# U of the gated layer made in the layer's row blocks, and two bfloat16 parts made by ScalarE

## What is computed

```
Wh = x @ W_w + W_b
Uh = x @ U_w + U_b
Vh = x @ V_w + V_b
out_src = Wh * attn_l
out_dst = Wh * attn_r
sigma = jax.nn.sigmoid(out_src[src] + out_dst[dst])
sum_sigma_h = jax.ops.segment_sum(Vh[src] * sigma, dst, num_segments=N)
sum_sigma = jax.ops.segment_sum(sigma, dst, num_segments=N)
h = Uh + sum_sigma_h / (sum_sigma + 1e-06)
```

## Time and profile before

| | us |
|---|---|
| median of 3 runs | 3004.75 (3004.15 to 3007.91) |
| the profiled execution | 3003.86, its span 3002.2 |
| input stage, first gather to last subtraction | 1639.3 to 1732.8 |
| gather stage, first gather to last store | 1738.4 to 2817.9 |
| last stage | 2830.0 to 3002.2 |

### The profile page before, as it was taken

One profiled execution on the slowest core, in us unless ns is written; L12 is line 12 of the kernel. 1 busy time (PEld: TensorE's weight loads), 2 busy tenths in 40 slices (PEclk: granted clock), 3 DMA queues, 4 the chain that ended last, 5 costly groups with the idle time before them and its releaser, 6 DMA issues. The chain is left out here.

```text
span 3002.2 us, 50772 instructions
## 1 busy us (share of the span) xinstructions
PE 2495.9 (83%) x17111; PEld 1245.4 (41%) x17164; DVE 2350.3 (78%) x5375; ACT 1158.3 (39%) x2327; POOL 1364.5 (45%) x1627
## 2 busy tenths in 40 slices
PE   5999979999969999966997947677676777767598
PEld 3666655333355333344665512233332333323365
DVE  6888889999959999977444847777777777777477
ACT  5777720000020000012222435666666666566421
POOL 2999920000000000001830867777777777775055
PEclk8999989999989999976998977888888888888799
DMA  4000000000020000031432687888888888888343
GB/s 125 12 11 12 10 36 15 15 15 15 5 82 15 15 15 15 5 100 45 121 96 64 203 249 238 250 259 256 259 255 252 257 257 260 255 252 250 121 150 107
DMA packets 210756, 373.53 MB, mean 124 GB/s; under 512 B 52554, under 2 KB 140559, under 8 KB 208682
## 3 DMA queue, kind: packets, MB, share of 16 engines
q0 software_dynamic: 75536, 238.14, 26.4%
q1 hardware_dynamic: 131737, 128.66, 13.5%
q10 hardware_dynamic: 3200, 3.21, 0.4%
HBM read 324.84 MB, written 50.04 MB: 125 GB/s over the span
## 5 line engine op out<-in xcount | busy, mean ns | idle before, releaser
L1167 PE MATMUL dense_p_o<-dense_W,feat 128*32 128x512 f32 x7200 | 789.8, 595 | 17.5 <-DVE dense_W L1099 17.5
L1099 DVE SCALAR_TENSOR_TENSOR dense_W<-layer_B,steep,cnt 128x512 f32<-128x512 f32 x1200 | 796.7, 750 | 3.3 <-DVE dense_W L1099 2.0
L2466 POOL DMA_INDIRECT Wd<-tab_d,ixq x544 | 519.4, 955 | 171.1 <-issue 166.2
L1167 PEld LDWEIGHTS dense_p_o<-dense_W,feat 128*32 128x32 f32 x7200 | 281.9, 110 | 494.5 <-issue 390.3
L1577 POOL MEMSET edst<- 128x782 int32 x1 | 0.8, 750 | 921.9 <-POOLq L1216 921.9
L2644 PE MATMUL strips_p_sg<-strips_sv,strips_oh 128*32 128x512 f32 x2000 | 313.6, 704 | 101.0 <-DVE strips_sv L2509 101.0
L2632 PE MATMUL strips_p_b<-strips_wrs,strips_ohT 96*128 96x256 bf16 x1000 | 177.8, 308 | 208.8 <-DVE strips_ohT L2480 190.6
L732 POOL TENSOR_SCALAR mix_L<-mix_back,encode_lowT 128x128 bf16<-128x128 f32 x520 | 328.6, 650 | 18.7 <-PE mix_p_c L891 18.6
L2573 ACT ACTIVATE strips_p_s<-strips_tv 128x1024 f32<-128x1024 f32 (+1 forms) x250 | 225.2, 901 | 157.3 <-DVE strips_sv L2509 144.5
L1123 ACT COPY dense_part<-dense_p_o 128x512 f32<-128x512 f32 x36 | 18.8, 596 | 639.7 <-PE dense_p_o L1167 639.7
L2466 POOL DMA_INDIRECT strips_G<-tab_d,ixq x240 | 228.9, 954 | 73.1 <-issue 72.8
(11 more groups left out here) (543 smaller groups left out, 3899.3 us busy)
## 6 DMA issues: line engine op xcount, KB each, us to landing
strips_row<-dlr_d SPq DMA_DIRECT2D x250, 96.0 KB
ew<-in_ew SPq DMA_DIRECT2D x16, 1024.0 KB, 5.4
layer_B<-rise_d SPq DMA_DIRECT2D x12, 1024.0 KB, 4.6
hx_d<-hrow SPq DMA_DIRECT2D x24, 512.0 KB, 2.7
Wd<-tab_d,ixq POOLq DMA_INDIRECT x544
Wd<-in_fWd SPq DMA_DIRECT2D x8, 1024.0 KB, 9.2
tab_d<-feat SPq DMA_DIRECT2D x50, 130.0 KB, 1.9
tab_d<-gated_in_rowg SPq DMA_DIRECT2D x25, 256.0 KB, 2.0
```

Of the source, the lines that this page charges most:

```text
L1099: o = nc.vector.scalar_tensor_tensor(out=out, in0=rise, scalar=C.steep[:, q * H + h:q * H + h + 1], in1=count, op0=ALU.max, op1=ALU.mult)
L1167: m = nc.tensor.matmul(p_o[c % 2][h * MT:(h + 1) * MT, a, 0:n], feat[:, q, h, lo:lo + MT], W[t % 3][:, h, 0:n], start=(q == 0), stop=(q == ...
L2466: gp.indirect_dma_start(out=G[n % RING][:, j, :], out_offset=None, in_=C.tab3[:, :], in_offset=bass.IndirectOffsetOnAxis(ap=index, axis=0) ...
```

## The change

- **Input stage.** `w3` holds only W and V, loaded in two pieces. U's product, its copy `us` and its store are gone; the second product has 256 columns. The transposed rows `xT` get four buffers and SP stores them to `xT_d` (`turned`), ahead of the block's `row`. VectorE no longer multiplies by attn_r twice. ScalarE makes part 0 by a cast of `wf` (`first_part`, two rounds behind) and part 1 by another cast of `wf` after GpSimd's first subtraction (`second_part`, three rounds behind). GpSimd keeps the two subtractions, each waiting for one of the casts.
- **Gather stage.** `wu` holds U's weights. `project(b)` makes U of block b in the last 256 columns of `p_h`: two matmuls from `xTu` and a bias matmul, on TensorE at the end of the block's steps, behind the gate matmuls of block b-2. VectorE adds it from PSUM. SP loads `xTu` (one buffer) when the product of the block before is done. `xn` has one buffer, the zero matmuls read `b3S` in place of `nil`, and waits keep the last part of `p_h` apart from the hidden layer.
- **The branch not taken** gets a loop that makes U for all blocks.

```diff
-        w3 = sb("w3", [P, KC, 3 * D])
+        w3 = sb("w3", [P, KC, 2 * D])
...
+                def turned(b):
+                    sp.wait_ge(s_tc, b + 1)
+                    sp.dma_start(C.xT_d[ds(b * P, P), :], xT[b % 4][:, :]).then_inc(s_xTd[b % 4], 16)
...
                     k = b % 3
-                    gp.wait_ge(s_row, b * 3 + 3)
+                    gp.wait_ge(s_w0, b + 1)
                     nc.gpsimd.tensor_tensor(wf[k][:, :], wf[k][:, :], wp[k][:, 0, :], ALU.subtract).then_inc(s_sp, 1)
-                    gp.wait_ge(s_sp, b * 3 + 1)
-                    nc.gpsimd.tensor_copy(wp[k][:, 1, :], wf[k][:, :]).then_inc(s_sp, 1)
-                    gp.wait_ge(s_sp, b * 3 + 2)
+                    gp.wait_ge(s_w1, b + 1)
                     nc.gpsimd.tensor_tensor(wp[k][:, 2, :], wf[k][:, :], wp[k][:, 1, :], ALU.subtract).then_inc(s_sp, 1)
...
-                    nc.vector.tensor_tensor(wp[m][:, 0, :], p_a[k][:, 0, 0:D], ar[:, :], ALU.mult).then_inc(s_row, 1)
...
-                    nc.scalar.copy(row[k][:, D:2 * D], p_a[k][:, 1, D:2 * D]).then_inc(s_pass, 1)
-                    nc.scalar.copy(us[k][:, :], p_a[k][:, 1, 0:D]).then_inc(s_pass, 1)
+                    nc.scalar.copy(row[k][:, D:2 * D], p_a[k][:, 1, 0:D]).then_inc(s_pass, 1)
+
+                def first_part(b):
+                    act.wait_ge(s_row, b * 2 + 2)
+                    if b >= 3:
+                        act.wait_ge(s_wd[b % 3], 16 * (b // 3))
+                    nc.scalar.copy(wp[b % 3][:, 0, :], wf[b % 3][:, :]).then_inc(s_w0, 1)
+
+                def second_part(b):
+                    act.wait_ge(s_sp, b * 2 + 1)
+                    nc.scalar.copy(wp[b % 3][:, 1, :], wf[b % 3][:, :]).then_inc(s_w1, 1)
...
-                for b in range(NB + 1):
+                for b in range(NB + 3):
...
-                    if b >= 1:
+                    if 1 <= b <= NB:
                         taken(b - 1, (b - 1) % 2)
+                    if 2 <= b <= NB + 1:
+                        first_part(b - 2)
+                    if b >= 3:
+                        second_part(b - 3)
...
-                    for a, lo, w in ((0, 0, D), (1, D, 2 * D)):
+                    for a, bias in ((0, 0), (1, 2 * D)):
...
                     def load_u(b):
-                        sp.dma_start(U[b % 2][:, :], C.u_d[b * P:(b + 1) * P, :]).then_inc(s_u[b % 2], 16)
+                        if b >= 1:
+                            sp.wait_ge(s_up, b)
+                        sp.dma_start(xTu[:, :], C.xT_d[b * P:(b + 1) * P, :]).then_inc(s_u, 16)
...
-                        if i == 0 and b >= 1 and b + 1 < NB:
-                            sp.wait_ge(s_ur, b)
+                        if i == 8 and 0 <= b and b + 1 < NB:
                             load_u(b + 1)
...
-                            v.wait_ge(s_u[b % 2], 16 * (b // 2 + 1))
+                            v.wait_ge(s_up, b + 1)
                             v.wait_ge(s_d, 4 * b + 2)
-                            nc.vector.tensor_tensor(h, h, U[b % 2][:, :], ALU.add).then_inc(s_ur, 1)
+                            nc.vector.tensor_tensor(h, h, p_h[:, F - D:F], ALU.add).then_inc(s_ur, 1)
...
+                    def project(b):
+                        if b == 0:
+                            pe.wait_ge(s_wu, 16)
+                            pe.wait_ge(s_ones, 1)
+                        else:
+                            pe.wait_ge(s_ur, b)
+                        pe.wait_ge(s_u, 16 * (b + 1))
+                        for kc in range(KC):
+                            nc.tensor.matmul(p_h[:, F - D:F], xTu[:, kc * P:kc * P + P], wu[:, kc, :], start=(kc == 0), stop=False)
+                        nc.tensor.matmul(p_h[:, F - D:F], ones[:, :], C.b3S[:, D:2 * D], start=False, stop=True).then_inc(s_up, 1)
...
+                            if i == QC + 7 and b < NB - 1:
+                                pe.wait_ge(s_ur, b + 2)
...
                             t.then_inc(s_l4, 1)
+                            if b + 2 < NB:
+                                project(b + 2)
                         if i == 2 * QC + 2:
                             pe.wait_ge(s_lt, b + 1)
+                            pe.wait_ge(s_ur, min(b + 3, NB))
```

More of the change, by code:

```diff
@@ L2148, in _ @@
                     sp.wait_ge(s_wd[k], 16 * ((NB + 2 - k) // 3))
+                for k in range(4):
+                    sp.wait_ge(s_xTd[k], 16 * ((NB + 3 - k) // 4))
                 sp.wait_ge(s_dw, 32)
-                sp.wait_ge(s_rowd[0], 32 * ((NB + 1) // 2))
-                sp.wait_ge(s_rowd[1], 32 * (NB // 2))
+                sp.wait_ge(s_rowd[0], 16 * ((NB + 1) // 2))
+                sp.wait_ge(s_rowd[1], 16 * (NB // 2))
             @block.gpsimd
@@ L2654, in group @@
                             for n in range(4):
-                                nc.tensor.matmul(p_sg[g // QC % 2][:, :], nil[:, 0:P], nil[:, :], start=False, stop=False)
+                                nc.tensor.matmul(p_sg[g // QC % 2][:, :], nil[:, :], C.b3S[:, 0:2 * D], start=False, stop=False)
                         sums(g)
+                    def project(b):
[8 more added lines that the diff above has]
+                        nc.tensor.matmul(p_h[:, F - D:F], ones[:, :], C.b3S[:, D:2 * D], start=False, stop=True).then_inc(s_up, 1)
                     def tail(b, i):
+                        if i == 0 and b < 2:
+                            project(b)
                         if i == QC + 4:
@@ L2940, in load_u @@
                         sp.dma_start(U[b % 4][:, :], C.u_d[b * P:b * P + P, :]).then_inc(s_u[b % 4], 16)
+                    sp.dma_start(wu[:, :, :], A["w3"][:, D:2 * D].rearrange("(c p) f -> p c f", p=P)).then_inc(s_wu, 16)
+                    for b in range(NB + 1):
+                        if b < NB:
+                            if b >= 2:
+                                sp.wait_ge(s_up, b - 1)
+                            sp.dma_start(U[b % 2][:, :], C.xT_d[b * P:b * P + P, :]).then_inc(s_ux[b % 2], 16)
+                        if b >= 1:
+                            sp.wait_ge(s_uc, b)
+                            sp.dma_start(C.u_d[(b - 1) * P:b * P, :], U[2 + (b - 1) % 2][:, :]).then_inc(s_us[(b - 1) % 2], 16)
+                    sp.wait_ge(s_us[0], 16 * ((NB + 1) // 2))
+                    sp.wait_ge(s_us[1], 16 * (NB // 2))
                     for b in range(4):
@@ L3042, in _ @@
                 with when_even(C, act, 0):
+                    for b in range(NB):
+                        act.wait_ge(s_up, b + 1)
+                        if b >= 2:
+                            act.wait_ge(s_us[b % 2], 16 * (b // 2))
+                        nc.scalar.copy(U[2 + b % 2][:, :], (p_l, p_r)[b % 2][:, 0:D]).then_inc(s_uc, 1)
                     def root(c):
@@ L3080, in _ @@
                 with when_even(C, pe, 0):
+                    pe.wait_ge(s_wu, 16)
+                    pe.wait_ge(s_ones, 1)
+                    for b in range(NB):
+                        pe.wait_ge(s_ux[b % 2], 16 * (b // 2 + 1))
+                        if b >= 2:
+                            pe.wait_ge(s_uc, b - 1)
+                        to = (p_l, p_r)[b % 2][:, 0:D]
+                        for kc in range(KC):
+                            nc.tensor.matmul(to, U[b % 2][:, kc * P:kc * P + P], wu[:, kc, :], start=(kc == 0), stop=False)
+                        nc.tensor.matmul(to, ones[:, :], C.b3S[:, D:2 * D], start=False, stop=True).then_inc(s_up, 1)
+                    pe.wait_ge(s_uc, NB)
                     pe.wait_ge(s_wd, 64)
@@ L3432, in build @@
             counts.close()
-            bias = ExitStack()
-            C.b3S = bias.enter_context(nc.sbuf_tensor("b3S", [ST, 3 * D], BF16, side="right"))
+            C.b3S = ctx.enter_context(nc.sbuf_tensor("b3S", [ST, 3 * D], BF16, side="right"))
             ahead = ExitStack()
@@ L3451, in build @@
             stage_gated_in(nc, C, A)
-            bias.close()
             C.Wd = ctx.enter_context(nc.sbuf_tensor("Wd", [P, NE * FC * D], F32, side="right"))
```

79 lines of the change are left out of this document (42 added, 37 removed).

## The result

| | before | after |
|---|---|---|
| median of the runs, us | 3005.18 (3004.15 to 3007.91, 4 runs) | 3045.89 (3043.73 to 3048.34, 4 runs) |
| the profiled execution, its span | 3003.86, 3002.2 | 3045.38, 3043.7 |

The changed kernel takes 1.0134 times as long, with a 95% interval of 1.0117 to 1.0152. The forecast was 3013.6 us, with a range of 3003 to 3028 us: the direction was right, the size was not.

A forecast was written before the change was run, and what follows sets the result against it. Four nearly level queues were taken to bound the input stage, GpSimd's gathers the gather stage. 3003.86 + 7.3 (input stage) + 1.2 (SP's wait) + 0.3 (drain) = 3012.7, with 0.9 for the median 3013.6 us; range 3003 to 3028.

The forecast's parts named there:

- way round the loop: Input stage: VectorE, ScalarE's casts, GpSimd's subtraction and next gather wait in a ring; 7.51 us for two blocks.
- SP's wait: Gather stage: SP's transposed-rows load waits for U's product, strip-index loads behind it; VectorE 0.2 to 1.2 us late, +1.2 us.
- the slack: Gather stage: lateness a block can absorb while GpSimd's gathers set the pace, 1.3 us, read from the last block.
- Gather to landing: Input stage, a leg of the ring: from the gather's start to its data landing, median 3.2 us, least 2.7.
- Start to normalisation: Input stage, a leg of the ring: from VectorE's start of a block to ScalarE's normalisation, 1.64 us.
- The upper bound of the text, 8.5 us: Input stage: two blocks' time if casts last as long as the normalisation and the start is held to 2.09 us.
- The sentence on shared ports: Input stage: two-SBUF-input VectorE and SBUF-reading GpSimd instructions exclude each other; met every block, 7.96 us, stage 4 us later.
- The tail of the stage: Input stage, from block 24's start to the last subtraction's end: 14.2 us instead of 13.5, +0.7.
- rival 3: Gather stage: SP's lateness exceeds what a block absorbs, 1.9 us a block, 14 us more, 3027 us; chance 0.10.
- Rival 4: Input stage: TensorE's clock may fall to 1.2 GHz, 4.4 us a block, up to 12 us, 3020 with half; chance 0.10.
- Rivals 1 and 2: Input stage: ring does not bind, 2995 us, chance 0.10; or ring at its lower bound 7.0 us, 3008 us, chance 0.15.
- the engine sums: Input stage: a block's time from each engine's own work alone, without the ring of waits, 2.7 to 2.9 us.

The follow-up runs named there:

- e2: Changed kernel with ScalarE's two casts at the head of its input-stage round instead of the end; 3030.14 us, 1.008 times the kernel before.
- e7: Changed kernel with SP's transposed-rows load five strip-index loads later and GpSimd's split seven blocks behind the gather instead of six; 3009.22 us, one run.
- e4: Changed kernel with SP's transposed-rows load later, no casts on ScalarE, VectorE's third multiply and GpSimd's cast back; 3000.38 us, 0.998 times the kernel before.
- e6: Changed kernel with SP's transposed-rows load later and VectorE's offset operation written with one tensor input and two scalars; 3025.49 us, one run.
- e5: Changed kernel with SP's transposed-rows load later and TensorE making V's two matmuls twice in the input stage; 3035.32 us, one run.
- e3: Changed kernel with both edits: SP's transposed-rows load later, ScalarE's casts at the head of its round; 3004.49 us, 0.9989 times the kernel before.
- e8: Changed kernel with later transposed-rows load, casts at the head of ScalarE's round, GpSimd's second subtraction behind the next gather; 2999.42 us, 0.9974 times before.
- e1: Changed kernel with SP's load of the transposed rows five strip-index loads later in the gather stage; 3022.86 us, 1.0058 times the kernel before.

## Why the prediction was right, and where it was wrong

The forecast was 32 us too low, and two of its terms were mis-sized. For the input stage it had 7.3 us, and 19.6 were measured, since a way round the loop took 8.6 us and not 7.51. For SP's wait it had 1.2 us, and the gather stage grew by 21.1 us, since the strip-index load was late by more than the slack in 18 blocks and not in the last alone. A block pace over 41.7 us in the gather stage was one of the text's own signs of being wrong; it is 42.50 us.

- **What bounds the input stage, and which loop the casts close: right.** The order of waits, the idle time on GpSimd's second subtraction (32.9 us in 19 places) and on ScalarE's root, and VectorE waiting for the gather are as foretold; opened at either of two places (e2, e7), the loop no longer sets the pace. Block 6 was forecast 2.5 us earlier; measured from the first add it starts 13.5 us on, where it was 16.5.
- **The way round, "7.51 us for two blocks": wrong by 1.1 us.** Over nine times round that is 10 of the 11 us by which 78.7 us from block 6 to block 24 exceed the forecast's 67.5. Two terms carry most of it. *Gather to landing*, 3.2 us from the earlier trace rows, was 3.84 us. That is a mean over 17; the median is 3.66 us, and the last five, with one of 5.74 us, lift it. VectorE was idle before 16 of the 17 adds, so nearly all of it is the landing. (The profile tells the landing itself for 7 of the 25 gathers only, 3.5 to 4.0 us; the add of 1690.55 above stands 3.17 us behind its gather.) The earlier trace rows is a median over all 25 blocks, in which VectorE waited for one gather (6.0 us). It hides a drift: the landings of blocks 8 to 13 took 2.8 to 3.0 us there, those of blocks 18 to 24 3.5 to 3.9. Why the adds of blocks 7 to 12 start 3.6 to 3.7 us behind their gathers in the loop, with less DMA traffic (158 to 186 GB/s after, 216 to 226 before), is left open. Being waited for can't be the whole reason: in e4 VectorE waits for none of the gathers from block 7 on, and the five of these whose landing the profile tells took 3.5 to 4.7 us. *Start to normalisation*, 1.64 us from block 1, was taken from a block ahead of GpSimd's first subtraction. With subtractions about, it was 1.65 to 2.45 us. The upper bound of the text, 8.5 us, was the better forecast, though half by luck: it held the start and the casts to be slow, and not the landing.
- **The sentence on shared ports: the traces bear its rule out, in part.** In the profile of after VectorE's add takes 0.85 us beside a GpSimd subtraction (1682.30 beside 1682.20) and 0.48 alone, and the offset operation 0.59 beside one (1684.12 beside 1684.01) and 0.16 alone. The Trainium skill (SBUF — State Buffer, Who interferes with whom) says that such a pair excludes each other, and that a VectorE instruction with at most one SBUF input, outside the 2-port modes, doesn't contend. This case's runs agree: in e6 the form with one tensor input took 212 to 215 ns everywhere. Subtractions aren't the whole of it, though: of the nine adds over 0.55 us in the profile of after, four began while GpSimd issued a gather, ahead of its next subtraction, up to 0.99 us at 1703.86. What held those is open. By the rule the text priced a way round of 7.96 us if every block met it. It was met in part of them, and the leg grew by 0.26 us on average, not 0.45.
- **The tail of the stage, "14.2 us": 15.7.** From block 24's add at 1738.99 to the end of the last subtraction at 1754.0 + 0.67. With both edits it is still 13.7 us, and with no casts on ScalarE 11.0, so the casts, taken in turn with the subtractions, keep the drain long.
- **SP's wait: the mechanism was right, its term of 1.2 us was not.** This was rival 3, with a chance of 0.10, a lateness of 1.9 us and 14 us in all. Measured were waits of 45.0 us in 21 places, 2.1 us each, and +21.1 us. The step that failed is the sum "2428.7 to 2429.7, and with a landing of 4.2 us". From the gate matmuls to the issue of the strip-index load it allowed 2.4 to 3.4 us and was given 3.48: the product ran for 2.08 us, twice the 1.03 of the earlier trace rows, and the bias matmul for another 0.42. Then the landing took 4.9 us rather than the median 4.2. Against the text's upper 1.2 us of lateness that is 0.1 us by the issue and 0.7 by the landing. Over the stage the mask came 5.1 us behind the issue in the median; why that is longer than 4.2 the runs don't tell. The slack was read well (1.3 us; 1.0 to 1.27 measured), and it is exactly what makes the term steep: each tenth of a microsecond of lateness beyond it costs 2.4 us. With a nominal lateness up to 1.2 and a worst of 2.8 around a threshold of 1.3, the forecast took the side without cost for every block but the last. Rival 3 deserved a chance well above 0.10.
- **Rival 4, the clock: small.** The granted clock did fall, from 1.00 to 0.92 and 0.93. As a price of its own it is some 3 us at most by the count above, of the waits in which TensorE stands in the loop; e5 didn't settle it closer. In e4 the clock stayed at 1.00 with TensorE busy for three quarters of the time.
- **Rivals 1 and 2: wrong as stated.** The loop binds well above 7.2 us. The 2.9 us a block of rival 1, and the 2.7 to 2.9 us of the engine sums, aren't reached even where the loop is opened: a block takes 3.28 to 3.31 us in e2 and e3 and 3.06 us with GpSimd's split skewed. The engine sums took 0.64 us off GpSimd for its cast (0.70 by the text's own reading of the rows) and put the wait for ScalarE's cast in its place at nothing; it is 0.51 us.
- **The drain, "0.3 us", and the last stage: no fault found**, +0.1 us from the last tenth step's add to the end. Over the ten kernels of the experiments that stretch is 212.1 to 216.9 us, so a term of 0.3 us can't be told from nothing.

The range left out that both stages could fall on their bad side together. The text's own ends, 17.7 us for the input stage and 14 us for SP's wait, with 0.3 for the drain and 0.9 for the median, make 3036.8 us; with 21 us in place of the 14 it is 3044.

## What to carry to other kernels

- Before work is handed to an engine with room, write out the ring of waits that the hand-over closes, and count how many blocks share one time round it. Here the same casts cost 22 us at the end of ScalarE's round and 4 us at its head: the place in the list, and not the load of the engine, was the price.
- A load behind a wait in a queue that other loads share is a wait for all of them. Put it where what it waits for has long happened, even if that is later than it could go out; one place in the list was worth 19 us of the gather stage here (23 us of the whole time), and one the other way cost 185 us of it (175 us of the whole).
- Where a cost is only felt beyond a slack, compare its whole spread with the slack and multiply by the blocks. If the threshold lies inside the spread, that is a case with a large chance and not a small term in the sum.

## What the runs showed of the hardware

- A round trip GpSimd, ScalarE, GpSimd with a cast of 128x256 took 0.51 to 0.52 us of GpSimd's time in 18 of 25 blocks of e3 and up to 2.6 us in the others, against 0.70 us for its own cast in the middle of the stage before. Here, handing over one short step in the middle of a chain gave back almost nothing until the order was skewed as well (e8).
- An operation on 128x1 values, 0.16 us alone, took up to 0.60 us beside a GpSimd subtraction (after, e1); with a scalar in place of its second tensor, 0.21 us everywhere (e6).
- In three stretches of the input stage the granted clock of TensorE, a mean between its levels of 1.2 and 2.4 GHz, was 1.00 with 44.54 of 59 us busy (e4), 0.97 with 46.96 of 59 us busy (e3) and 0.86 with 56.23 of 79 us busy (after, 1656 to 1735 us). The forecast had tied a fall of the clock to TensorE no longer being busy throughout; e4's row doesn't bear that out.
